# Between two attentions: work taken chunk by chunk, half of the projections moved behind the start of the gated scores, and the quotients taken out

## The reference

```python
# block 0: rope attention, then a quantised net
x = x + (attention0(x) @ Wo0)                    # each block adds its normalised output
h = layernorm(x) * g0 + b0
x = x + residual + 0.5 * (silu(h @ w1 + fb1) @ w2 + fb2)
# block 1, gated attention, 16 heads of 8
x = (sequence - mean) / sqrt(var + EPS) * ln_gamma + ln_beta
q, k, v = heads(x @ Wq.T + bq), heads(x @ Wk.T + bk), heads(x @ Wv.T + bv)
scores = einsum('bhqd,bhkd->bhqk', q, k) / sqrt(8)
scores = sigmoid(scores - mu) * exp(scores)
scores = scores / sum(scores, -1)
out = einsum('bhqk,bhkd->bhqd', scores, v) @ Wo.T + bo
```

## Time and profile before

| | us |
|---|---|
| median of 3 executions | 1476.43 |
| lowest, highest | 1474.38, 1478.0 |
| the profiled execution's own time | 1478.0 |
| its span, first to last instruction | 1476.2 |
| its mean granted PE clock | 0.954 |
| PE, DVE, ACT busy | 1264.9, 1129.2, 1121.5 |
| from 290 to 360.9, between the attentions: PE, DVE, ACT busy of 70.9 | 52.6, 39.2, 41.7 |
| from 360.9 to 852.9, the gated attention: PE, DVE, ACT busy of 492.0 | 406.1, 388.4, 478.1 |

### The profile page before, as it was taken

One profiled execution on the slowest core, in us unless ns is written; L12 is line 12 of the kernel. 1 busy time (PEld: TensorE's weight loads), 2 busy tenths in 40 slices (PEclk: granted clock), 3 DMA queues, 4 the chain that ended last, 5 costly groups with the idle time before them and its releaser, 6 DMA issues.

```text
span 1476.2 us, 22855 instructions
## 1 busy us (share of the span) xinstructions
PE 1264.9 (86%) x8290; PEld 655.0 (44%) x8290; DVE 1129.2 (76%) x2049; ACT 1121.5 (76%) x1604; POOL 351.2 (24%) x434
## 2 busy tenths in 40 slices
PE   6699999895788788888888898988999988888996
PEld 3344444362111111111111146666777766566874
DVE  8888987456787978877758778597766686777898
ACT  4178877756999999999999945654576567778885
POOL 2500001642000000001100037553546548340000
PEclk9599999997799999999999999999999999999998
DMA  6300110003100000100000030023333233011111
GB/s 193 116 24 24 35 36 4 2 1 111 47 22 1 22 22 1 38 1 22 22 0 1 1 151 1 1 62 92 101 94 109 77 117 121 29 36 29 43 45 57
DMA packets 41088, 70.50 MB, mean 48 GB/s; under 512 B 6416, under 2 KB 14864, under 8 KB 40208
## 3 DMA queue, kind: packets, MB, share of 16 engines
q1 hardware_dynamic: 40976, 69.05, 15.0%
HBM read 59.26 MB, written 9.76 MB: 47 GB/s over the span
## 4 chain that ended last, share of the span: by engine, by line
PE 33%; DVE 26%; ACT 20%; issue 13%; POOL 4%; DMA 1%; SPq 1%; POOLq 0%; ACTq 0%; DVEq 0%
ACT SHARED L1140 12%; DVE SHARED L1176 8%; PE PS L823 5%; PE PS L787 3%; DVE PS L2350 2%; PE PS L2140 2%; PE PS L645 2%; PE PS L2142 2%; PE PS L2141 2%; PE PS L1366 2%; PE PS L712 2%; PE PS L2149 2%; PE PS L2146 1%; PE PS L2147 1%; DVE X L284 1%
## 5 line engine op out<-in xcount | busy, mean ns | idle before, releaser
L1140 ACT ACTIVATE SHARED<-PS 128x1536 f32<-128x1536 f32 (+1 forms) x346 | 457.6, 1450 | 15.9 <-PE PS L1036 10.0
L1176 DVE TENSOR_TENSOR SHARED<-SHARED 128x1536 f32<-128x1536 f32 (+1 forms) x170 | 276.6, 1704 | 34.7 <-ACT SHARED L1140 34.7
L1036 PE MATMUL PS<-QS,KS 48*128 48x512 bf16 (+1 forms) x1006 | 208.6, 398 | 84.7 <-ACT SHARED L1140 77.2
L803 ACT ACTIVATE SHARED<-PS 128x512 f32<-128x512 f32 (+3 forms) x384 | 163.6, 493 | 72.6 <-PE PS L791 64.1
L1036 PEld LDWEIGHTS PS<-QS,KS 48*128 48x128 bf16 (+1 forms) x1006 | 38.5, 95 | 298.7 <-ACT SHARED L1140 269.2
L2140 PE MATMUL PS<-ROUNDED 128*128 128x512 f32 x328 | 139.1, 424 | 15.6 <-DVE ROUNDED L2337 9.2
L1049 PE MATMUL PS<-SHARED,Vg 128*16 128x512 f32 x1024 | 137.1, 609 | 4.7 <-DVE SHARED L1176 4.3
L732 DVE TENSOR_REDUCE NM<-PS 128x2 f32<-128x1024 f32 (+3 forms) x128 | 124.1, 1020 | 13.0 <-PE PS L718 12.3
L2142 PE MATMUL PS<-ROUNDED 128*128 128x512 f32 x328 | 130.8, 399 | 0.0
L2141 PE MATMUL PS<-ROUNDED 128*128 128x512 f32 x328 | 130.6, 398 | 0.0
L2270 ACT ACTIVATE ROUNDED<-PS 128x512 fp32r<-128x512 f32 x100 | 59.8, 598 | 91.3 <-DVE PS L2350 89.6
(11 more groups left out here) (279 smaller groups left out, 2473.4 us busy)
## 6 DMA issues: line engine op xcount, KB each, us to landing
SHARED<-wx SPq DMA_DIRECT2D x64, 256.0 KB, 3.1
SHARED<-in_moe SPq DMA_DIRECT2D x3, 1600.0 KB, 11.1
SHARED<-wx SPq DMA_DIRECT2D x16, 224.0 KB, 2.9
SHARED<-kx SPq DMA_DIRECT2D x32, 96.0 KB
KS<-kx SPq DMA_DIRECT2D x32, 96.0 KB
SHARED<-wx SPq DMA_DIRECT2D x16, 192.0 KB, 2.8
SHARED<-wx SPq DMA_DIRECT2D x16, 160.0 KB, 2.7
qx<-SHARED SPq DMA_DIRECT2D x16, 128.0 KB, 2.4
```

The source lines that it names most:

```text
L803: act.activation(PB[t % 3][:, h, q0:CH], bank(RING0[n % 3], q0), ACT.Exp, scale=SCORE_SCALE)\
L1036: ins = pe.matmul(bank((v % 2) * GRP + f - a), KS[g % 2][r, h // 2, kt * P:kt * P + P], QS[g % 2][r, h // 2, qh * CH:(qh + 1) * CH], start ...
L1140: act.activation(dst, PS[:, (v % 2) * GRP * CH:((v % 2) * GRP + b - a) * CH], ACT.Exp if second == qh else ACT.Sigmoid, scale=SCORE_SCALE)\
L1176: dve.tensor_tensor(ex_tile(j), ex_tile(j), GR[w % RING][:, 0:(b - a) * CH], ALU.mult)\
```

## The change

Between the attentions each engine's list is woven anew, chunk by chunk. PE enters the gated scores with the queries, keys and values of chunks 0 and 1 alone; values and projections of chunks 2 and 3 are inside the first pass (n = 0), on PE behind tiles 1, 2, 4, 5, 7 and 8, and their copies and parts on DVE, chunk 3's parts after the first half's products. Their PSUM banks are 6 and 7. PE waits for chunk 3's turn on edge 2 instead, and has 20 and 12 filler matmuls before it. SP's order of the writes is by chunk and part mixed. No half has a quotient.

```diff
-        QKB = (3, 1)
-        def pe_qkv1(pe, c):
+        QKB = ((3, 1), (3, 1), (6, 7), (6, 7))
+        def pe_values1(pe, c):
             pe.wait_ge(h_ready, edges[2].n_x(c))
             pe_values(pe, 1, c, RW["bv1"])
-            if c:
-                pe.wait_ge(A[1, "qf"], 2 * c)
-            pe.matmul(bank(QKB[0]), W[:, WM["q1"], :], chunk(hT, c), start=True, stop=True)
-            pe.matmul(bank(QKB[1]), W[:, WM["k1"], :], chunk(hT, c), start=True, stop=True)\
+        def pe_project1(pe, c, m):
+            pe.wait_ge(h_ready, edges[2].n_x(c))
+            if c % QH:
+                pe.wait_ge(A[1, "qf"], 2 * (c - 1) + m + 1)
+            pe.matmul(bank(QKB[c][m]), W[:, WM[("q1", "k1")[m]], :], chunk(hT, c), start=True, stop=True)\
...
+        def act_project1(act, c, m):
+            act.wait_ge(A[1, "proj"], 2 * c + m + 1)
+            act.activation(QKF[c % 2][m], bank(QKB[c][m]), ACT.Identity, bias=col(("bq1", "bk1")[m]))\
+               .then_inc(A[1, "qf"], 1)
+        def dve_project1(dve, c, m):
+            dve.wait_ge(A[1, "proj"], 2 * c + m + 1)
+            dve.tensor_scalar(QKF[c % 2][m], bank(QKB[c][m]), col(("bq1", "bk1")[m]), None, ALU.add)\
+               .then_inc(A[1, "qf"], 1)
+        def dve_values1(dve, c):
+            dst = Vall[:, :].rearrange("p (b g k e) -> p b g k e", b=B, g=HG, k=KT)
+            dve.wait_ge(A[1, "vt"], c + 1)
+            dve.wait_ge(A[1, "vall"], c)
+            k0 = (c % QH) * TPC
+            dve.tensor_copy(dst[:, c // QH, :, k0:k0 + TPC, :],
+                            bank(4 + c).rearrange("p (k g e) -> p g k e", k=TPC, g=HG)).then_inc(A[1, "vall"], 1)
...
-        QUOTIENT = (0, 2, 4, 6, 8, 14)
...
-        def by_quotient(n, j):
-            return n % 2 == 1 and n // 2 in QUOTIENT and j == 0
-        SCORED = [(n, j) for n in range(4 * NG) for j in range(NTILE) if not by_quotient(n, j)]
+        SCORED = [(n, j) for n in range(4 * NG) for j in range(NTILE)]
...
+        def pe_keep_clock_before(pe, count):
+            pe.wait_ge(x_sum, edges[2].n_y(2))
+            for a in range(count):
+                pe.matmul(bank(6), identb[:, :], masks[:, 0:CH], start=True, stop=True)
...
+            if n == 0 and j in (1, 2):
+                pe_values1(pe, QH + j - 1)
+            if n == 0 and j in (4, 5):
+                pe.wait_ge(A[1, "vall"], QH + j - 3)
+                pe_project1(pe, QH, j - 4)
+            if n == 0 and j in (7, 8):
+                pe_project1(pe, QH + 1, j - 7)
...
+        def dve_before_gated(dve):
+            dve_values1(dve, 2)
+            dve_values1(dve, 3)
+            dve_project1(dve, 2, 0)
+            dve_project1(dve, 2, 1)
+            dve_part0(dve, 1, 2)
+            rest_of_part0(dve, 1, 2)
+            dve_project1(dve, 3, 0)
+            dve_project1(dve, 3, 1)
+            dve_part1(dve, 1, 2)
+            part2(dve, 1, 2)
         def dve_beside_gated(dve, own, hf):
+            if hf == 1:
+                dve_part0(dve, 1, 3)
+                rest_of_part0(dve, 1, 3)
+                dve_part1(dve, 1, 3)
+                part2(dve, 1, 3)
...
         def dve_gated(dve, own):
-            dve.wait_ge(A[1, "part2"], 2 * NC)
-            dve_quotient_begin(dve, own, 0)
+            dve_before_gated(dve)
             for hf in range(QH * NG):
-                if hf in QUOTIENT:
-                    dve_quotient_end(dve, own, hf)
                 for j in range(NTILE):
-                    if by_quotient(2 * hf + 1, j):
...
+                pool.wait_ge(A[1, "vall"], QH if g < HG else NC)
                 pool_group_values(pool, 1, g, g % 2)
...
-            sp_stack_first(sp, 1, [(c, part) for part in range(3) for c in range(QH)])
+            sp_stack_first(sp, 1, ((0, 0), (0, 1), (1, 0), (0, 2), (1, 1), (1, 2)))
...
+            pe_ffn_unit(pe, 1, FW1, 0)
+            pe_ffn_unit(pe, 1, FW1, 1)
             pe.wait_ge(A[0, "a_red"], NG * (NMAX + 1 + QH))
             pe_turn_out(pe, 0, 2, 0)
+            pe_ffn_unit(pe, 1, FW1, 2)
+            pe_out_y(pe, 0, 2, "o0", None, 6)
             pe_turn_out(pe, 0, 3, 2)
-            pe_ffn_up(pe, 1, e1, FW1, 1)
-            pe_out_y(pe, 0, 2, "o0", None, 6)
+            pe_ffn_unit(pe, 1, FW1, 3)
             pe_out_y(pe, 0, 3, "o0", None, 7)
+            pe_ffn_unit(pe, 1, FW1, 4)
+            pe_ffn_unit(pe, 1, FW1, 5)
+            pe_ffn_unit(pe, 1, FW1, 6)
+            pe_ffn_unit(pe, 1, FW1, 7)
             pe.wait_ge(cbase, NBASE + 1)
             pe_ffn_down(pe, 1, FW2, HID0, RW["fc2b"], 0)
+            pe_turn_x(pe, e1, 2)
             pe_ffn_down(pe, 1, FW2, HID0, RW["fc2b"], 1)
-            pe_turn_x(pe, e1, 2)
+            pe.wait_ge(h_ready, e1.n_x(2))
+            pe_ffn_unit(pe, 1, FW1, 8)
+            pe_ffn_unit(pe, 1, FW1, 9)
             pe_turn_x(pe, e1, 3)
-            pe_ffn_up(pe, 1, e1, FW1, 2)
-            pe_ffn_up(pe, 1, e1, FW1, 3)
+            pe_ffn_unit(pe, 1, FW1, 10)
+            pe_ffn_unit(pe, 1, FW1, 11)
+            pe.wait_ge(h_ready, e1.n_x(3))
+            pe_ffn_unit(pe, 1, FW1, 12)
+            pe_ffn_unit(pe, 1, FW1, 13)
             pe_ffn_down(pe, 1, FW2, HID0, RW["fc2b"], 2)
             pe_turn_x(pe, e2, 0)
+            pe_ffn_unit(pe, 1, FW1, 14)
+            pe_ffn_unit(pe, 1, FW1, 15)
+            pe_turn_x(pe, e2, 1)
+            pe.wait_ge(A[1, "f_act"], 4 * NC)
+            pe_project1(pe, 0, 0)
+            pe_project1(pe, 0, 1)
+            pe_project1(pe, 1, 0)
+            pe_project1(pe, 1, 1)
             pe_ffn_down(pe, 1, FW2, HID0, RW["fc2b"], 3)
-            pe_turn_x(pe, e2, 1)
-            pe_qkv1(pe, 0)
-            pe_qkv1(pe, 1)
+            pe_values1(pe, 0)
             pe_turn_x(pe, e2, 2)
+            pe_values1(pe, 1)
+            pe_keep_clock_before(pe, 20)
             pe_turn_x(pe, e2, 3)
-            pe_qkv1(pe, 2)
-            pe_qkv1(pe, 3)
+            pe_keep_clock_before(pe, 12)
...
-            ffn(0)
-            act_attention_end(act, 0, (0, 2))
-            ffn(1)
+            def silu(u):
+                act_ffn_unit(act, 1, u, HID0, ACT.Silu, lambda m: col("s1", m), lambda m: col("fb1", m))
+            silu(0)
+            act_attention_end(act, 0, (0, 2), (2,))
+            silu(1)
+            silu(2)
+            act_attention_end(act, 0, (0, 2), (3,))
+            silu(3)
+            silu(4)
+            silu(5)
+            silu(6)
+            silu(7)
             act_apply(act, e1, 2)
+            act_turned(act, e1, 2)
             act_apply(act, e1, 3)
-            act_turned(act, e1, 2)
+            act.wait_ge(y_ready, YB[1] + 1)
+            silu(8)
+            silu(9)
             act_turned(act, e1, 3)
-            ffn(2)
+            silu(10)
+            silu(11)
             act_apply(act, e2, 0)
-            ffn(3)
+            act.wait_ge(y_ready, YB[1] + 2)
+            silu(12)
+            silu(13)
             act_apply(act, e2, 1)
             act_turned(act, e2, 0)
+            silu(14)
+            silu(15)
             act_turned(act, e2, 1)
-            act_qkv1(act, 0)
-            act_part0(act, 1, 0)
-            act_qkv1(act, 1)
-            act_part0(act, 1, 1)
+            act_project1(act, 0, 0)
+            act_project1(act, 0, 1)
+            act_part0(act, 1, 0, (0,))
+            act_part0(act, 1, 0, (1,))
+            act_project1(act, 1, 0)
+            act_part1(act, 1, 0, (0,))
+            act_part1(act, 1, 0, (1,))
+            act_part0(act, 1, 1, (0,))
+            act_project1(act, 1, 1)
+            act_part0(act, 1, 1, (1,))
+            act_part1(act, 1, 1, (0,))
+            act_part1(act, 1, 1, (1,))
             act_apply(act, e2, 2)
-            act_part1(act, 1, 0)
-            act_part1(act, 1, 1)
+            act.wait_ge(x_sum, e2.n_y(1))
+            act_values(act, 1, 0)
             act_turned(act, e2, 2)
+            act_values(act, 1, 1)
             act_apply(act, e2, 3)
             act_turned(act, e2, 3)
-            act_values(act, 1, 0)
-            act_values(act, 1, 1)
-            act_qkv1(act, 2)
-            act_qkv1(act, 3)
-            act_values(act, 1, 2)
-            act_values(act, 1, 3)
...
             dve_y(dve, own, e1, 2)
+            dve_x(dve, own, e1, 2)
             dve_y(dve, own, e1, 3)
-            dve_x(dve, own, e1, 2)
             dve_x(dve, own, e1, 3)
+            dve_keep(dve, own, e1, 2)
             dve_y(dve, own, e2, 0)
             dve_y(dve, own, e2, 1)
             dve_x(dve, own, e2, 0)
             dve_x(dve, own, e2, 1)
-            dve_keep(dve, own, e1, 2)
+            dve_y(dve, own, e2, 2)
             dve_keep(dve, own, e1, 3)
-            dve_y(dve, own, e2, 2)
+            dve_x(dve, own, e2, 2)
+            rest_of_part0(dve, 1, 0, (0,))
+            rest_of_part0(dve, 1, 0, (1,))
+            part2(dve, 1, 0, (0,))
+            rest_of_part0(dve, 1, 1, (0,))
+            part2(dve, 1, 0, (1,))
+            rest_of_part0(dve, 1, 1, (1,))
```

(61 more changed lines are left out.)

53 lines of the change are left out of this document (5 added, 48 removed).

## The result

The changed kernel takes 1457.45 us (median of 4, 1452.54 to 1458.33) against 1477.22 (median of 4, 1474.38 to 1479.33) for the kernel before in the same session: ratio 0.987, 95% interval 0.9857 to 0.9883, faster by 19.8 us. A second measurement in a later session gave 1456.93 (4 runs), ratio 0.9861 (0.9846 to 0.9877).

The account below looks back on a forecast made before the run. ACT was taken to bound the gated stage, and DRAM writes and loads its start. Terms -12.2 + 2.5 + 1.3 - 3.5 = -11.9 us, against the median 1476.43, gave 1464.5 us, range 1458.0 to 1470.5.

Parts of the forecast that it names:

- First write 326.2, last 335.8, gap-free: Between the attentions: SP's 16 writes would run without gaps, first at 326.2 instead of 336.44, last at 335.8 instead of 348.07.
- Chunk 3 turned by 343.4: Before the gated scores: chunk 3's turn would end at 343.4, 5 us before the loads.
- Term -12.2 for the start: Start of the gated stage: earlier writes let PE start at 348.7 instead of 360.90, -12.2 us, bounds -13.5 and -9.
- Term +2.5, half clock for the first 5 us: First pass: added values and projections run at PE's half clock for 5 us, costing 2.5 us, bounds 0.3 and 9.2.
- PE keeps its clock: Rival at the start: fillers hold PE's clock over the wait, giving 1460.6 us; chance 0.15.
- Term +1.3 for the first stretch's waits: First pair of passes: 33 tiles instead of 32 with the old 1.70 us of waits kept, +1.3 us.
- Term -3.5 for the quotients: Five later halves without their quotient: 0.70 us saved in each, -3.5 us in all, bounds -4 and -2.
- The two dips: Pass edges: two later stretches without quotient took 31.82 us instead of 30.26 at clock 0.95; the sum kept both.
- Chunk 3 becomes the gate: Rival before the stage: chunk 3 comes 8 us later, the start slips by 3, giving 1467.5 us; chance 0.12.
- Half clock all through: Rival in the first pass: PE stays at half clock, extras cost 9.2 instead of 2.5 us, giving 1471.2; chance 0.10.
- Slower, dips at the edges: Rival at pass edges: clock dips of 1.56 us each spread to as many as fifteen halves, up to 1484.8 us; chance 0.03.
- the removal of the quotients does nothing: Rival in the later halves: ACT's waits for DVE stay, so no gain; the prediction called it excluded, without a chance.

Follow-up runs that it names:

- e2: The changed kernel with the old lists of PE, ACT, DVE and POOL between the attentions and the old write order; 1471.82 us, ratio 0.9975 to the kernel before.
- e3: The changed kernel with values and projections of chunks 2 and 3 put back before the gated scores; 1463.44 us, ratio 0.9917 to the kernel before.
- e6: The changed kernel with SP's 16 writes in the old order (part by part over both chunks); 1461.51 us, ratio 0.9897 to the kernel before.
- e7: The kernel before, unchanged, run and profiled a second time; 1478.83 us (one run).
- e4: The changed kernel without the 20 and 12 filler matmuls before the start; 1459.10 us, ratio 0.9888 to the kernel before.
- e10: The changed kernel with the additions of e8 and e9 together; 1456.01 us, ratio 0.9859 to the kernel before.
- e8: The changed kernel with filler matmuls added on PE in the first two passes; 1457.07 us, ratio 0.9880 to the kernel before.
- e5: The changed kernel with quotients put back in halves 2, 4, 6, 8 and 14, with their late weight slots and extra fillers; 1463.07 us, ratio 0.9908 to the kernel before.
- e1: The kernel before with its six quotients removed and a wait for the last product behind the stage; 1471.81 us, ratio 0.9972 to the kernel before.
- e9: The changed kernel with the eight k writes on POOL's queue beside the eight q writes on SP's; 1455.46 us, ratio 0.9865 to the kernel before.
- e11: The changed kernel unaltered, on the same chip as e9 and e10, for comparison; stage time 542.04 us.

## Why the prediction was off by 8 us, point by point

- **First write 326.2, last 335.8, gap-free:** 325.94, 335.60, gap-free. Chunk 3 turned by 343.4: 342.96. The walk through the lists with the old durations held to 0.5 us over 35 us. e2, e3 and e6 show what carried it: undoing the orders costs 15.0, of it the writes' order 1.3; undoing the move behind the start costs 4.0, once the orders are there.
- **Term -12.2 for the start** measured -14.68. The prediction said that the rest of the string is the same. It was not: the last write landed in 2.39 us instead of 4.02, and that is luck, an unlucky profile of the kernel before (e7). Another 0.4 is attention 0, another 0.4 the first tile, at full clock now. Against e7, both from the end of attention 0, it is 56.96 - 69.71 = -12.75.
- **Term +2.5, half clock for the first 5 us:** measured 0. **This is a step that failed.** I took it from the earlier trace rows that the wait before the start costs the clock, and had the fillers done by 345 and PE idle until 348.7. The clock did fall behind PE's wait for chunk 3's apply (2.62 us; 0.51 from 342.8 to 346.1). But at half clock the fillers last twice as long, which stretched them to 346.42, to the end of the wait for the loads, and with PE busy all that time the clock was back by the first tile (0.99 from 346 to 350). e4, without them, shows the forecast's case at 2.0 us, and 0.4 in the first tile. The Trainium skill (TensorE: Matmul & The Clock Gate, section "Why this matters for your kernels") advises against idle gaps between bursts of matmuls, since they send the clock to the lower level. The change's trace agrees with it for that wait, e10's doesn't: there PE waited 2.68 us at the same place and the clock stayed at 1.00. The rival *PE keeps its clock*, at 1460.6, was nearer in number than the forecast, but its mechanism is e10's and not the change's: here the clock was lost and regained.
- **Term +1.3 for the first stretch's waits:** +0.92. The wait named at 387.11 stayed, as 1.24 us at 372.44; e8 shows that it is the clock's.
- **Term -3.5 for the quotients:** the five halves gave -3.77, within the bounds, but the 0.70 for each was an average with the half of 30.33 us behind the first dip. e5 puts a quotient at 0.89, five at 4.46, outside the bounds. The first dip and the half behind it took 62.14 us where e5 takes 61.30, so that dip cost 0.84 net, and the second 1.48. Both splits give the same 6.8.
- **The two dips went as well, -3.04 as the windows stand, 2.3 net, and this is the other step that failed:** I priced the dips only as a risk that could spread, on the ground that fillers and thin edges were alike, and kept both in the sum. e1 and e5 show them to belong to the kernels with quotients. Why they stood at these places, why e7 has a third and e5 just the second, stays open. The prediction's "over ten dips" to be slower is eight by its own numbers (11.9 / 1.56), and ten only with the 4.4 us of noise on top.
- *Chunk 3 becomes the gate:* no. The loads ended last, but the margin of 5 us shrank: chunk 3 was turned at 342.96, its fillers ended at 346.42, just as the loads landed. With two queues (e9) they cost 0.1 us at most.
- *Half clock all through* and *Slower, dips at the edges* are refuted by the windows; *the removal of the quotients does nothing* by e1 and e5.

The differences from forecast to measured, -2.48 (start), -2.5 and -0.38 (first stretch), -0.27, -3.04 and +0.03 (later stretches), -0.46 (behind), give the 9.1 between -11.9 and -21.0. The range was set by adding the kept clock to the forecast; it had no place for dips that end.

## What to carry to other kernels

When a change shortens the way to a stage, ask what was hidden in the old wait (here 4 us of projections), and move that as well. Fillers on PE placed between the last hand-over and the data can be worth more than their time says: in the change they stretched over the wait at half clock and handed the stage a full clock, 2.4 us by e4. And count a disturbance that only the removed work's neighbourhood shows as a possible gain too, not only as a risk.

## What the runs showed of the hardware that was not expected

- Two queues issue sixteen writes of 128 KB in 6.9 us (e9, 325.23 to 332.11) instead of 10.3 (the change, 325.94 to 336.20), but the DMA engines then are the limit: 291 GB/s and a share of 0.96 between 332 and 336 in e10, where one queue holds 203 GB/s and 0.73 in e11. The median landing of the writes grows from 2.4 us to 3.3 to 3.6.
- The same twelve fillers took 4.44, 3.73 and 2.75 us in three kernels that differ little ahead of them (change, e9, e10). PE waited 2.62 us in the change and 2.68 in e10 before chunk 3's transpose; the granted clock fell to 0.51 in the change and stayed at 1.00 in e10. The fillers' end moved with it, the start hardly did, since the loads set it.
- Ten loads issued alike: from the last one's issue to the landing of all it took 3.0 to 4.0 us over thirteen profiles (e8 3.01, change 3.30, e9 3.89, e4 3.99), and where the loads set the start, it moves by as much.
